# Attention in a two-layer gated cross-attention kernel: the row maxima of both halves in one turned tile, subtracted by products of 256 columns in place of 128

## The reference, cut to what matters

```python
q = q.reshape(B, T, H, D).transpose(0, 2, 1, 3)      # 16 heads of 16 features
att = jnp.einsum('bhtd,bhid->bhti', q, k) * (1.0 / np.sqrt(D))
att = jax.nn.softmax(att, axis=-1)                   # over the 77 rows of the context
y = jnp.einsum('bhti,bhid->bhtd', att, v)
...
scores = jnp.einsum('bhtd,bhsd->bhts', q, k) + bias  # the second attention
weights = jax.nn.softmax(scores, axis=-1)
attn = jnp.einsum('bhts,bhsd->bhtd', weights, v)
```

## Time and profile before

| | |
|---|---|
| median of three runs | 1925.44 us (1922.43 to 1928.44) |
| profiled execution, its own time | 1927.09 us |
| its span, first to last instruction | 1925.3 us |
| TensorE matmul busy | 1747.5 us (91%) |
| weight loads (in the shade of matmuls) | 1487.9 us (77%) |
| VectorE, ScalarE, GpSimd busy | 1058.9, 717.5, 731.8 us |
| mean granted TensorE clock | 0.967 of full speed |

### The profile page before, as it was taken

How to read it: one execution, slowest core, us unless ns; L and a number is a source line. 1 busy time by engine, 2 the same in 40 slices (tenths; PEclk the granted TensorE clock), 3 DMA queues, 4 the chain that set the end, 5 groups by cost and what they waited for, 6 DMA issues and landing times.

```text
span 1925.3 us, 42924 instructions
## 1 busy us (share of the span) xinstructions
PE 1747.5 (91%) x13746; PEld 1487.9 (77%) x13747; DVE 1058.9 (55%) x2921; ACT 717.5 (37%) x1401; POOL 731.8 (38%) x1002
## 2 busy tenths in 40 slices
PE   5899998999989999899899998985399999999997
PEld 3787877877778787787787777874288888888886
DVE  2465656656566565665665656655444444444443
ACT  1332323333333332333332333324245555555553
POOL 3133334334343333434434344243134443444443
PEclk9999999989999999999998999988699999999999
DMA  4310101101011010110111101022544444444443
GB/s 115 69 39 17 37 25 45 32 21 37 25 45 37 17 36 25 45 37 18 45 26 35 37 19 45 23 88 82 141 74 69 72 70 73 69 74 68 68 74 42
DMA packets 174252, 96.99 MB, mean 50 GB/s; under 512 B 103056, under 2 KB 167952, under 8 KB 174224
## 3 DMA queue, kind: packets, MB, share of 16 engines
q1 hardware_dynamic: 147344, 60.88, 13.0%
q0 software_dynamic: 26880, 35.73, 11.3%
HBM read 44.77 MB, written 46.76 MB: 48 GB/s over the span
## 4 chain that ended last, share of the span: by engine, by line
PE 62%; issue 16%; POOL 12%; DVE 4%; ACT 3%; DMA 1%; SPq 1%; POOLq 0%; ACTq 0%; DVEq 0%
PE bank L1449 23%; PE scores L1449 12%; POOL sorted_rows L1069 4%; PE bank L1639 4%; PE scores L1639 3%; PE bank L1505 3%; PE scores L1596 2%; POOL rstd L1008 2%; PE scores L1699 2%; PE bank L1699 2%; POOL x L1017 2%; PE scores L1583 2%; PE scores L1682 2%; ACT routed L1162 1%; PE scores L1621 1%
## 5 line engine op out<-in xcount | busy, mean ns | idle before, releaser
L1086 POOL DMA_INDIRECT out<-y,ids x144 | 224.1, 1556 | 345.6 <-DMA out<-y,ids 202.2
L1433 DVE SCALAR_TENSOR_TENSOR h<-scores,relu 128x512 f32<-128x512 f32 x144 | 99.5, 691 | 292.2 <-ACT relu L1183 248.6
L1124 ACT ACTIVATE turned_x<-bank 128x512 f32<-128x512 f32 x160 | 95.5, 597 | 369.8 <-PE bank L1505 368.6
L1301 DVE TENSOR_REDUCE mx<-scores 128x16 f32<-128x1232 f32 x128 | 183.5, 1434 | 70.9 <-PE scores L1564 70.2
L1449 PE MATMUL bank<-w,turned_x 128*128 128x256 f32 x768 | 204.3, 412 | 10.6 <-ACT turned_x L1124 10.5
L1008 POOL TENSOR_TENSOR rstd<-var,half_power 128x2 f32<-128x2 f32 x96 | 67.8, 706 | 320.5 <-DVE var L1257 320.2
L1449 PEld LDWEIGHTS bank<-w,turned_x 128*128 128x128 f32 x768 | 148.2, 203 | 35.1 <-ACT turned_x L1124 12.9
L1449 PE MATMUL bank<-down_hi,ht_hi 128*128 x576 | 174.6, 303 | 0.1
L1069 POOL DMA_INDIRECT sorted_rows<-routed,place x128 | 129.2, 1009 | 111.0 <-ACT routed L1162 44.0
L1449 PE MATMUL bank<-down_hi,ht_lo 128*128 x576 | 162.4, 282 | 0.0
L1449 PE MATMUL bank<-down_lo,ht_hi 128*128 x576 | 162.3, 282 | 0.0
(11 more groups left out here) (203 smaller groups left out, 4080.9 us busy)
## 6 DMA issues: line engine op xcount, KB each, us to landing
xe<-sorted_rows SPq DMA_DIRECT2D x72, 257.0 KB
x_new<-x_rows SPq DMA_DIRECT2D x32, 256.0 KB, 2.7
out<-x_end SPq DMA_DIRECT2D x32, 256.0 KB, 2.2
raw<-w_up_t SPq DMA_DIRECT2D x8, 512.0 KB, 5.7
raw<-w_down_t SPq DMA_DIRECT2D x8, 512.0 KB, 5.8
ctx<-ctx_t SPq DMA_DIRECT2D x32, 77.0 KB
vb<-v_rows SPq DMA_DIRECT2D x64, 38.5 KB
sorted_rows<-zero_rows SPq DMA_DIRECT2D x9, 257.0 KB
```

Of the source, the lines that this page charges most:

```text
L1086: pool.indirect_dma_start(out=acc, out_offset=bass.IndirectOffsetOnAxis(ap=ids[j][:], axis=0), in_=y[j][:], in_offset=None, compute_op=ALU ...
L1124: act.activation(turned_x[u][:].rearrange("p k t -> p (k t)"), bankA[:], ACT.Copy).then_inc(sem(f"t_ready{u}"), 1)
L1301: dve.tensor_reduce(mx[u][:, g, :, 0:2 * NC], sc[:, 0:NJ, 0:NC * PK].rearrange("p j (h s) -> p j h s", s=S), AX.X, ALU.max).then_inc(sem(f ...
L1433: dve.scalar_tensor_tensor(out=h[j % 2][:], in0=sc[:, 2 + j % 2, :], scalar=0.0, in1=relu[j % 2][:], op0=ALU.max, op1=ALU.mult)\
```

## The change

The maxima of both halves now lie in one tile of 136 columns: row `32 j + 8 c + 4 e + g` of the turned tile is the maximum of head pair `j`, token block `c`, head `e` of the pair and half `g`. The transposes are taken per token block `c` in place of per half `g`; the second one reads the tile from column 8 on, so that both blocks put a half's maxima on the same partitions. `neg_mx` then holds 256 tokens side by side for every head, and one product with 256 columns does what two with 128 did.

```diff
-    expand = np.zeros((P, NC, PK + REST))
+    expand = np.zeros((P, G, PK + REST))
     for j in range(NJ):
-        for c in range(NC):
+        for g in range(G):
             for e in range(2):
-                expand[2 * DH * j + 2 * c + e, c, e * S:(e + 1) * S] = 1
-            expand[2 * DH * j + 2 * c + 1, c, PK + j * RK:PK + (j + 1) * RK] = 1
+                expand[2 * DH * j + 4 * e + g, g, e * S:(e + 1) * S] = 1
+            expand[2 * DH * j + 4 + g, g, PK + j * RK:PK + (j + 1) * RK] = 1
...
-        mx = [sb1(f"mx{u}", [P, G, NJ, 2 * DH]) for u in range(2)]
-        neg_mx = [sb1(f"neg_mx{u}", [P, G, P], F32R) for u in range(2)]
+        mx = [sb1(f"mx{u}", [P, NJ * 2 * DH + 8]) for u in range(2)]
+        neg_mx = [sb1(f"neg_mx{u}", [P, NC, P], F32R) for u in range(2)]
...
-                dve.tensor_reduce(mx[u][:, g, :, 0:2 * NC], sc[:, 0:NJ, 0:NC * PK].rearrange("p j (h s) -> p j h s", s=S),
+                dve.tensor_reduce(mx[u][:, 0:P].rearrange("p (j r) -> p j r", j=NJ)[:, :, 0:8 * NC].rearrange("p j (h r) -> p j h r", r=4)[:, :, :, g], sc[:, 0:NJ, 0:NC * PK].rearrange("p j (h s) -> p j h s", s=S),
                                   AX.X, ALU.max).then_inc(sem(f"mx_ready{u}"), 1)
...
-                for g in range(G):
-                    last = pe.transpose(sc[:, 4, g * P:(g + 1) * P], mx[u][:, g].rearrange("p j r -> p (j r)"), ident[:])
+                for c in range(NC):
+                    last = pe.transpose(sc[:, 4, c * P:(c + 1) * P], mx[u][:, 8 * c:8 * c + P], ident[:])
...
                 for g in range(G):
-                    for c in range(NC):
-                        for j in range(NJ):
-                            rows = slice(2 * DH * j, 2 * DH * (j + 1))
-                            last = pe.matmul(sc[:, j, g * T + c * P:g * T + (c + 1) * P], expand[rows, c, 0:P], neg_mx[u][rows, g],
-                                             start=False, stop=g == G - 1 and c == NC - 1)
+                    for j in range(NJ):
+                        rows = slice(2 * DH * j, 2 * DH * (j + 1))
+                        last = pe.matmul(sc[:, j, g * T:(g + 1) * T], expand[rows, g, 0:P], neg_mx[u][rows].rearrange("p c t -> p (c t)"),
+                                         start=False, stop=g == G - 1)
...
-                    for c in range(NC):
-                        last = pe.matmul(sc[0:REST, 4, g * T + c * P:g * T + (c + 1) * P], expand[:, c, PK:PK + REST], neg_mx[u][:, g],
-                                         start=False, stop=g == G - 1 and c == NC - 1)
+                    last = pe.matmul(sc[0:REST, 4, g * T:(g + 1) * T], expand[:, g, PK:PK + REST], neg_mx[u][:].rearrange("p c t -> p (c t)"),
+                                     start=False, stop=g == G - 1)
```

More of the change, by code:

```diff
@@ L135, in build @@
         fft_in = sb1("fft_in", [P, 4, NK, D])
-        expand_raw = sb1("expand_raw", [P, NC, PK + REST])
+        expand_raw = sb1("expand_raw", [P, G, PK + REST])
         hot_raw = sb1("hot_raw", [32, LINE])
@@ L170, in build @@
         ffn_row = sb1("ffn_row", [P, D])
-        expand = sb1("expand", [P, NC, PK + REST], F32R)
+        expand = sb1("expand", [P, G, PK + REST], F32R)
         ident_b = sb1("ident_b", [P, P], BF16)
@@ L1134, in max_turned @@
                 act.wait_ge(sem(f"max_turned{u}"), num(t, 2, l + 1))
-                act.activation(neg_mx[u][:].rearrange("p g t -> p (g t)"), sc[:, 4, 0:G * P], ACT.Copy, scale=-1.0).then_inc(sem(f"neg_mx_ready{u}"), 1)
+                act.activation(neg_mx[u][:].rearrange("p c t -> p (c t)"), sc[:, 4, 0:T], ACT.Copy, scale=-1.0).then_inc(sem(f"neg_mx_ready{u}"), 1)
             def exp(t, u, l, n):
```

## The result

The changed kernel takes 1941.7 us (median of four runs, 1940.0 to 1945.7), the one before 1923.9 us in the same comparison: ratio 1.0086, interval 1.0068 to 1.0105. It is slower by 0.9%, 17.8 us, and lies outside the stated range of 1908 to 1938.

The account below looks back on a forecast made before the run. TensorE was taken to set the pace. From the profiled 1927.1 us, 9.0 saved work came off and 8.3 for slowed rounds went on, giving 1926.4, stated as 1924 in terms of the median; range 1908 to 1938.

Parts of the forecast that it names:

- The work: TensorE's products in less_max and by_key_rest: 16.6 us saved in all, of which 9.0 us reaches the end.
- The burst of `less_max`: Maxima subtracted by 256-column products: 0.35 us in place of 0.49, a saving taken as 0.15 us.
- the sum: Whole-kernel total: 1927.1 us, less 9.0 for saved work, plus 8.3 for the clock.
- two products of `by_key_rest`: Pair of 256-column products: 0.24 us in place of 0.30, saving 0.11 us for both halves.
- One reading under it: Old less_max burst of sixteen 128-column products: each four take some 0.12 us, no cheaper than four of 256.
- The share that reaches the round: Per round, three less_max and one by_key_rest savings survive TensorE's waits: 0.56 us.
- The waits for `xn`: TensorE's waits ahead of transposes: expected to swallow nearby savings, growing by 0.1 and 0.25 us.
- its stepped output: Reduction writing its maxima with a step of four elements: priced at zero, upper bound 4.5 us.
- the clock term: Slowed rounds of the loop: seven of 14 in place of five, at 4.2 us each, +8.3 us.
- Rival B: Many more rounds slowed by the clock: ten of 14 gives 1937 us, twelve 1946; chance 0.20.
- The size of a slowed round: Extra time of a loop round at reduced granted clock: 4.2 us each.
- the beat: Round length against something looking at TensorE at its own times: a round shorter by 0.56 us changes it.

Follow-up runs that it names:

- e8: Changed kernel with only less_max wide, by_key_rest back to two products of 128 columns for each half: 1943.7 us.
- e12: Kernel before, with unused 512-column products in two TensorE waits, four ahead of the transposes and two ahead of by_query: 1908.4 us.
- e9: Changed kernel, with unused 512-column products in two TensorE waits, four ahead of the transposes and two ahead of by_query: 1899.4 us.
- e7: Kernel before, with two of eight low-half bias products for sequence 1 left out, so a shorter round: 1940.3 us.
- e4: Kernel before, with one unused 512-column product added ahead of rows_by in each round: 1918.0 us.
- e1: Changed kernel, with three unused products (512, 512, 128 columns) added ahead of rows_by in each round: 1922.2 us.
- e2: Changed kernel, with unused 512-column products in two TensorE waits, three ahead of the transposes and two ahead of by_query: 1909.2 us.
- e3: Kernel before, with unused 512-column products in two TensorE waits, three ahead of the transposes and two ahead of by_query: 1908.7 us.
- e10: Changed kernel, both waits filled with four and two unused 512-column products, plus two more ahead of sequence 1's gate products: 1906.9 us.

## Why the prediction was wrong

**The work was right.** The burst of `less_max` costs 0.34 us (forecast 0.35; the sum took a saving of 0.15), two products of `by_key_rest` 0.23 (0.24). One reading under it was rough: 0.12 us for each four of the sixteen products is a mean. In the trace the starts of such a burst (607.26) lie in steps of 0.06, 0.11 and 0.11 us, and 0.21 pass from the last four to the next stage; the new burst has 0.12 and 0.21. The share that reaches the round is 0.54 us against 0.56: three `less_max` (0.43) and one `by_key_rest` (0.11), by e8. The waits for `xn` took the rest, by 0.07 and 0.26 us in the rows shown. The reduction kept its time (1.433 us against 1.430), so zero was the right price for its stepped output. Where the clock takes hardly a part, e12 and e9 differ by 9.0 us, the 9.0 of the sum. So close a match is luck: each ratio has an interval of 4 to 5 us either way. The firmer number is the 0.53 us between their rounds.

The Trainium skill, "TensorE: Matmul & The Clock Gate", section "Back-to-back issue gap", had by its isolated gap next to no saving, 112 against 109 ns for a pair. The same section says that this figure leaves out the weight load at few columns, and such products are what the change removes. The trace bears that out: four of 128 columns, one for each group of 32 rows, took 0.11 us behind the first step, almost as long as four of 256 (0.12).

**The step that failed is the clock term,** "I take half of the 14, seven, in place of five: 2 x 4.2 = +8.3 us". It was ten rounds and +17.7 us in the loop, and 2.8 us ahead of the loop, which the sum did not look at; at most 1.7 of these are a further fall. Rival B as priced, ten rounds, gave 1937, against 1941.7 measured; with the 2.8 us it would have been 1940. I gave it 0.20. The size of a slowed round was nearly right (3.85 against 4.2 us each), only their number was not. The prediction speaks of one fall in a slowed round; mostly there are two, the first of some 7 us and the second 24 us behind it.

What in the step was wrong is the choice of the middle, for which the prediction had no reason but that five and two-of-two lay on either side. It priced a change of the beat and not its direction. The runs show a direction: the rounds of e7 and e8, shorter by 0.43 us, pay for ten and eleven, as the changed kernel does, and those of e4, longer by 0.22 us, for two. That the kernel before might be well placed against a shorter round could be suspected from the earlier trace rows, where both rounds before it settled were slowed; the trace did not prove it. Whether a count can be worked out beforehand from the times of the falls was not tried. The range should have reached at least ten rounds plus what lies outside the loop.

**What is shown, and what stays open.** Shown: the count follows from changes of length that have nothing to do with the change and stand 30 and 48 us away from the fall (e4, e7); it does not hang on the wide products (e1); and it comes from the thin stretches (e2, e3, e9, e12: the rounds keep their length, and with the wait at the first place filled the falls there become fewer or cease). The run-to-run scatter is of the same kind: the kernel before ran from 1915.7 us (mean granted clock 0.975) to 1932.5 us (0.965) in 24 executions beside e1 to e4, a spread of four slowed rounds, e3 beside it from 1908.0 to 1911.2. So a difference of two or three slowed rounds between single profiles cannot be told from scatter: e1 and the kernel before, 78.30 and 78.26 us a round with two and five, are level by their medians (ratio 0.9989, 0.9969 to 1.0010).

Not shown is the rule by which a length gives a count. Over the lengths tried the count only falls as the round grows: 77.7 and 77.8 us give ten or eleven, about 78.3 two to five, 78.5 two. In these kernels a longer round is also one with more work in it, so they do not part the length from the share of work; that the same waits bring a fall in one round and none in the next, in regular turns, speaks for a beat. The falls outside the loop (in the last round from none in e10 to some 14 us at half clock in e1 and e2) were not tried, nor was a fill of the wait of 1.05 us.

## What to carry to other kernels

Where the profile shows a loop whose rounds come in two lengths at two granted clocks, count the slowed rounds before any small saving is judged: 0.5 us of saved work per round cost this kernel 18 us, and 0.2 us of added useless work gave it 7. Look for the thin stretch just ahead of the fall and fill its waits with products that nobody reads, into a bank that is about to be overwritten; then count again, since with falls left the two versions stood level (e2, e3) and with hardly any 9 us apart (e12, e9). And compare medians of several executions, since one profile shows one count of many. Here, for products that use 32 of the array's rows in four groups, four of 128 columns cost almost what four of 256 do, so a layout that lets one weight serve twice the columns took a third off such a burst (0.49 to 0.34 us).

## What the runs showed of the hardware that was not expected

- Half a microsecond less work in a round of 78 us doubled the rounds slowed by the clock (five of 14 to ten), by the change and by two products left out elsewhere (e7) alike.
- A fall at one thin stretch is mostly followed by a second at another 24 us later, and in the kernels whose waits were left as they were no round fell at the second alone.
- Unused products with an almost empty constant held the clock as well as ones with a dense table (1909.2 and 1909.1 us).
- One product of 512 columns more, in a wait that already had three, took the slowed rounds from six to two in the profiled executions (medians 1909.2 and 1899.4 us), at no cost in the round's length (77.72 us in both).
